# Two-layer cross-attention and experts: the order of the first attention's work on TensorE, in three blocks by the array's shape

## The chip, the cores and the metric
The kernel runs on one core of one Trainium2 chip, in one launch. The metric is device time in microseconds (us) of that core; the median of three runs of the kernel before is 792.72 us (792.16 to 794.59). Inputs and output are fp32.

## The reference, cut to what matters
```
x = x + L0_xattn(ctx, layernorm(x))        # the first attention: 16 heads of 64, 4 batches of 512 queries
x = x + L0_ffn(layernorm(x))               # 8 experts, each row to its best one
x = x + L1_xattn(layernorm(x), ctx)        # 16 heads of 8, keys from ctx alone
x = x + L1_ffn(layernorm(x))               # 8 experts, each row to its best two

def L0_xattn(ctx, latents):                # ctx (4, 32, 128), latents (4, 512, 128)
    kv_in = layer_norm(ctx), lat = layer_norm(latents)
    q = lat @ Wq                           # 128 -> 16 * 64
    k, v = concat([kv_in, lat]) @ Wkv      # 32 + 512 keys
    attn = softmax(q k^T / 8)              # exact, over 544 keys
    return (attn v) @ Wout
```
Only the first attention's order of work changes.

## The kernel before, in words
**Tiling.** The first attention is done pair by pair: two heads of 64 fill 128 partitions, 8 pairs per batch, 4 batches, so 32 pairs (`ALL`); four pairs are a group (`GROUP`), 8 groups. For a pair the kernel makes queries and keys (`qk`, six matmuls of 512 columns over the full 128x128 array, from rounded high and low parts), takes the maximum of each query's scores from the high parts alone (`top`: four tiles of 128 queries x 512 keys for two heads, and a fifth, `t4`, for the 32 context keys; DVE reduces each), turns the maxima into a row (`max_turn`, four transposes, full array; ACT keeps the row in `TOPROW`), makes the scores key tile by key tile (`scores`, four key tiles; each is four steps of two matmuls of 64 rows: high x high, high x low, low x high, and minus the maximum), ACT takes exp into `PT`, POOL adds the key tiles (`PSUMS`), and `pv` multiplies exp by the values (four key tiles, 64-column matmuls over 128 rows, into bank 6). `rows` sums over the keys on TensorE, once per two pairs, into bank 7.

Per group come `context_scores` (32 context keys, both heads, all four pairs, from an unrounded copy `QF` of the queries), `context_sums` and `context_add` (their part of the output, in two halves), `one_over` (the reciprocals of the sums, in four column quarters on DVE, split in a high and a low part by ACT and DVE), `spread` (the reciprocals brought to all partitions by TensorE, two pairs each, DVE multiplies), `out` (times Wout) and `add` (to x). Per batch: layernorm of the next batch (`a_stats`, `a_rstd`, `a_out`, `a_turn`, `a_split`), its `values` (four steps), and the routing of the finished batch (`r0_stats` to `r0_send`).

**The order.** It is written out by hand. `ITERATION` is a list of short names that is run for each pair i; in iteration i stand qk and the maxima of pair i+1 (`qk`, `t0` to `t4`, `mt`), pv of pair i-1 (`p0` to `p3`), the scores of pair i (`s0` to `s3`), and the slots (letters) in which `put` has placed the work of groups and batches. The result is one list, `order_a`; every engine runs its own part of each step in the order of this list, and the engines meet at semaphores. The last pair's rest stands in a list of its own, `rest`.

**Banks.** Each step named in `TAKES_BANKS` gets two PSUM banks, `2 * (place % 3)`, by turns: of three pairs of banks, a step uses the one that the third step before it used. TensorE waits (`claim`) until that one's reader is done: for `scores` ACT's exp, for `top` DVE's reduction, for `qk` DVE's low part of the queries (`QL`), for `max_turn` ACT's copy. `pv` and `rows` take no turning pair.

**Shapes.** A matmul's tile of the array stands in the profile behind the operation: 128*128 for qk, values, transposes, spread, out, r0_turn and r0_run; 128*64 for pv; 64*128 for top and scores; 128*32 for rows; 64*32 and 32*64 for the context.

Lines in the profile: L1407 to L1409 qk and values, L1569 and L1576 top (context: L1576), L1583 max_turn, L1602 scores, L1634 pv, L1689 spread; ACT L838 exp, L732 layernorm, L815 and L816 high parts, L863 the reciprocals' high part; DVE L1225 and L1228 low parts (KL, QL), L1235 and L1237 reductions of top, L1255 reciprocals; POOL L671 additions.

Of the kernel before, what the change touches and what calls it, by code (L numbers as in the profile page):

```python
# [13 lines left out]
P = 128  # L14
# [27 lines left out]
def build(nc, x, ctx, lnm_g, lnm_b, lnl_g, lnl_b, Wq, Wkv, Wout, rw, rb, w1, w2, cq, ckv, cc, Wr, Wg, Wu, Wd, out):  # L42
# [28 lines left out]
    with ExitStack() as stack:  # L71
# [35 lines left out]
        with ExitStack() as queries:  # L107
            QF = queries.enter_context(nc.sbuf_tensor("QF", [P, GROUP, S], F32))
            TOPROW = queries.enter_context(nc.sbuf_tensor("TOPROW", [P, GROUP, S], F32R))
# [47 lines left out]
        with ExitStack() as first:  # L157
            def sb1(name, *shape):
                return first.enter_context(nc.sbuf_tensor(name, [P, *shape], F32R))


            WH = sb1("WH", 3, INNER)
            WL = sb1("WL", 3, INNER)

            XTH = sb1("XTH", 2, S)
            XTL = sb1("XTL", 2, S)

            QH = sb1("QH", 2, S)
            QL = sb1("QL", 2, S)
            KH = sb1("KH", 2, S)  # L170
            KL = sb1("KL", 2, S)

# [82 lines left out]
        for b in range(B):  # L255
# [64 lines left out]
            "E A B PC CA0 C CA1 O0 ADD CS V qk p0 p1 t0 s0 t1 p2 t2 D s1 t3 p3 t4 P0 P2 s2 s3 rows mt O1 OUT "  # L320
            "O2 O3").split()
# [3 lines left out]
        def put(i, at, name, a):  # L325
            beside[i].setdefault(at, []).append((name, a))
        for g in range(2 * B):

            put(GROUP * g + GROUP - 1, "CS", "context_scores", g)
            for half in range(2 if g < 2 * B - 1 else 0):  # L330
                put(GROUP * (g + 1) + 1, "PC", "context_sums", (g, half))
                put(GROUP * (g + 1) + 1, f"CA{half}", "context_add", (g, half))
        for b in range(B + 1):
            i = b * PAIRS
            if 2 <= b:
                put(i, "A", "r0_slot", b - 2)
                put(i, "D", "r0_send", b - 2)
            if b == B:
                break
            if b + 1 < B:  # L340
                put(i, "E", "a_stats", b + 1)
                put(i, "A", "a_rstd", b + 1)
                put(i + 1, "D", "a_out", b + 1)
                put(i + 3, "C", "a_turn", b + 1)
                put(i + 3, "D", "a_split", b + 1)
                for kt in range(KT):
                    put(i + 4 + kt, "V", "values", (b + 1, kt))
            for g in (2 * b - 1, 2 * b):
                if g >= 0:

                    k = GROUP * (g + 1) + 1
                    for c in range(4):
                        put(k, f"O{c}", "one_over", (g, c))
                    put(k + 1, "P0", "spread", GROUP * g)
                    put(k + 1, "P2", "spread", GROUP * g + 2)
                    put(k + 1, "OUT", "out", g)
                    put(k + 2, "ADD", "add", g)
            if b > 0:
                put(i + 4, "E", "r0_stats", b - 1)
                put(i + 4, "A", "r0_rstd", b - 1)  # L360
                put(i + 4, "D", "r0_out", b - 1)
                put(i + 5, "D", "r0_turn", b - 1)
                put(i + 6, "B", "r0_logits", b - 1)
                put(i + 6, "C", "r0_top", b - 1)
                put(i + 7, "A", "r0_hot", b - 1)
                put(i + 7, "D", "r0_run", b - 1)
# [3 lines left out]
        order += first_top[4:] + [("max_turn", 0), ("context_kept", 1), ("counters", 0)]  # L370
# [17 lines left out]
        for at in ITERATION:  # L388
# [6 lines left out]
                ("one_over", (last, 0))] + [("pv", (ALL - 1, kt)) for kt in range(KT)]  # L395
        rest += [("one_over", (last, c)) for c in range(1, 4)] + [("context_sums", (last, 1), 4, 2), ("context_add", (last, 1)),
# [26 lines left out]
        SCORED = {step: i + 1 for i, step in enumerate(scored)}  # L423

# [3 lines left out]
        def context_of(g):  # L428
            return SCORED["context_scores", g]

# [297 lines left out]
        def scalar_program(act):  # L728
# [64 lines left out]
            for name, a, place, banks in order_a:  # L793
# [16 lines left out]
                elif name == "qk":  # L810
# [41 lines left out]
                elif name == "one_over" and a[1] == 0:  # L852
                    g = a[0]
# [63 lines left out]
        def vector_program(dve):  # L917
# [295 lines left out]
            for name, a, place, banks in order_a:  # L1213
# [26 lines left out]
                elif name == "max_turn":  # L1240
# [7 lines left out]
                elif name == "one_over":  # L1248
# [7 lines left out]
                    if c == 3:  # L1256
                        if g == 2 * B - 1:
                            tables(0, True, "rows")
                        dve.wait_ge(s_rech, g + 1)
                        dve.wait_ge(s_rec, 4 * (g + 1))  # L1260
                        dve.tensor_tensor(RECS[64:128, :], REC[0:64, :], RECS[0:64, :].bitcast(F32), ALU.subtract).then_inc(s_recl, 1)
# [125 lines left out]
        def tensor_program(pe):  # L1387
# [129 lines left out]
            for name, a, place, banks in order_a:  # L1517
# [87 lines left out]
                elif name == "context_scores":  # L1605
# [6 lines left out]
                    for step in range(2):  # L1612
                        if step:
                            pe.wait_ge(s_toprow, GROUP * (a + 1))
                        for p in range(GROUP):
                            for h in range(2):
                                r = slice(DH * h, DH * h + DH)
                                lhs = (KCF[r, half * GROUP + p, ctx_b], MINUS[r, 0:M].bitcast(F32))[step]
                                rhs = (QF[r, p, :], TOPROW[r, p, :].bitcast(F32))[step]
# [253 lines left out]
```

## Time and profile before
| | |
|---|---|
| median of 3 runs | 792.72 us |
| span of the profiled execution | 798.2 us |
| TensorE matmuls busy | 713.8 us (89%) |
| VectorE (DVE) | 491.6 us (62%) |
| ScalarE (ACT) | 366.9 us (46%) |
| GpSimd (POOL) | 378.2 us (47%) |

The profile is of one execution. Its span goes from the first to the last instruction; it is the only time of that execution that there is, and the profile adds nothing outside it. It is 5.5 us above the median of the runs, which were taken without the profiler. Busy time counts a matmul from its start to its modelled end, so neighbouring matmuls overlap: distances from start to start say what one costs. The first attention takes from about 15 to 515 us; behind it come the first experts, the second attention and its experts.

### The profile page before, as it was taken

The page shows a single profiled execution, that of the slowest core. Times are in us where ns is not written, and L with a number is a line of the kernel's source. Part 1 is how long each engine was busy: PE and PEld are TensorE (multiplying, and loading weights), DVE is VectorE, ACT ScalarE, POOL GpSimd, SP SyncE. Part 2 cuts the span into 40 slices and gives each one's busy share as a digit, 9 for nine tenths or more (in the row PEclk, how much of TensorE's full clock was granted, in tenths as well). Part 3 has the DMA queues.
Part 4 walks back from the last instruction along what each step waited for, and adds up shares of the span by engine and source line. Part 5 has one row for each costly group of instructions (what it writes and reads, how often), then busy time and mean ns, then how long its engine had stood idle before and what let it go on. Part 6 is the DMA issues. An engine that isn't in the chain of part 4 may idle for free.

```text
span 798.2 us, 13900 instructions
## 1 busy us (share of the span) xinstructions
PE 713.8 (89%) x4626; PEld 414.0 (52%) x4626; DVE 491.6 (62%) x1077; ACT 366.9 (46%) x572; POOL 378.2 (47%) x369
## 2 busy tenths in 40 slices
PE   4899999999999999999999999987995587659991
PEld 4655556545556545555545455454664244326660
DVE  4655484595594875675775666664442477746673
ACT  5465554564654553654554643432332543314440
POOL 6254453553563573464375454524222314765552
PEclk9999999999999999999999999999998688569996
DMA  9999999300000000000030004302111500122224
GB/s 235 163 161 160 158 160 157 43 1 1 1 2 1 6 10 1 1 1 2 1 119 1 1 1 106 119 18 58 36 39 56 174 2 28 37 72 67 81 69 177
DMA packets 69132, 50.45 MB, mean 63 GB/s; under 512 B 4068, under 2 KB 62312, under 8 KB 69064
## 3 DMA queue, kind: packets, MB, share of 16 engines
q1 hardware_dynamic: 65544, 42.30, 29.7%
q0 software_dynamic: 3520, 7.27, 2.8%
q8 instruction: 41, 0.67, 0.4%
q14 instruction: 27, 0.22, 0.1%
HBM read 20.07 MB, written 29.47 MB: 62 GB/s over the span
## 4 chain that ended last, share of the span: by engine, by line
PE 75%; DVE 8%; issue 6%; POOL 4%; ACT 3%; DMA 2%; another core or an unknown queue 1%; SPq 1%; DVEq 0%; POOLq 0%; ACTq 0%
PE PSUM L1602 14%; PE PSUM L1634 13%; PE PSUM L1444 7%; PE PSUM L1569 5%; PE PSUM L1469 4%; PE PSUM L1700 4%; PE PSUM L1403 4%; PE PSUM L1407 3%; PE PSUM L1409 2%; PE PSUM L1408 2%; PE PSUM L1583 2%; PE PSUM L1576 2%; PE PSUM L1620 2%; PE PSUM L1664 2%; POOL results_d L643 2%
## 5 line engine op out<-in xcount | busy, mean ns | idle before, releaser
L838 ACT ACTIVATE PT<-PSUM 128x1024 f32<-128x1024 f32 x128 | 128.7, 1025 | 134.2 <-PE PSUM L1602 133.9
L671 POOL TENSOR_TENSOR PSUMS<-PT 128x1024 f32<-128x1024 f32 x32 | 76.1, 2378 | 210.6 <-ACT PT L838 171.6
L671 POOL TENSOR_TENSOR PSUMS<-PSUMS,PT 128x1024 f32<-128x1024 f32 x62 | 149.7, 2415 | 16.6 <-ACT PT L838 9.7
L1235 DVE TENSOR_REDUCE TOPS<-PSUM 128x2 f32<-128x1024 f32 x128 | 152.0, 1220 | 7.4 <-PE PSUM L1569 7.0
L1634 PE MATMUL PSUM<-PT,BIG 128*64 128x512 f32 x512 | 130.6, 611 | 0.6 <-issue 0.6
L1444 PE MATMUL PSUM<-BIG,XGT 128*128 x170 | 86.5, 614 | 2.4 <-issue 1.6
L1225 DVE TENSOR_TENSOR KL<-PSUM,KH 128x512 fp32r<-128x512 f32 x32 | 22.1, 692 | 68.0 <-ACT KH L816 67.5
L1189 DVE TENSOR_TENSOR SIL<-SIL,PSUM 128x256 f32<-128x256 f32 (+1 forms) x62 | 32.1, 518 | 48.0 <-ACT SIL L758 45.4
L1569 PE MATMUL PSUM<-KH,QH 64*128 64x512 f32 x256 | 58.0, 449 | 3.9 <-DVE QL L1228 3.6
L1634 PEld LDWEIGHTS PSUM<-PT,BIG 128*64 128x64 f32 x512 | 28.4, 135 | 54.0 <-issue 52.5
L1602 PE MATMUL PSUM<-QH,KH 64*128 64x512 f32 x256 | 54.9, 424 | 1.0 <-DVE QL L1228 0.8
L1569 PEld LDWEIGHTS PSUM<-KH,QH 64*128 64x128 f32 x256 | 24.2, 183 | 59.2 <-DVE TOPS L1235 25.1
L758 ACT ACTIVATE SIL<-PSUM 128x256 f32<-128x256 f32 (+1 forms) x62 | 28.7, 463 | 55.1 <-PE PSUM L1444 43.5
L643 POOL DMA_INDIRECT results_d<-YS,IDX x39 | 37.4, 960 | 31.5 <-issue 20.4
L766 ACT ACTIVATE HIDT<-PSUM 128x256 f32<-128x256 f32 (+1 forms) x62 | 28.7, 463 | 51.3 <-PE PSUM L1403 43.0
L1602 PE MATMUL PSUM<-QL,KH 64*128 64x512 f32 x256 | 50.9, 390 | 0.0
L1602 PE MATMUL PSUM<-QH,KL 64*128 64x512 f32 x256 | 50.8, 390 | 0.0
L1602 PE MATMUL PSUM<-TOPROW,MINUS 64*128 64x512 f32 x256 | 50.7, 389 | 0.0
L643 POOL DMA_INDIRECT results_b<-YS,IDX x23 | 22.0, 956 | 47.1 <-DVE YS L1196 44.8
L1274 DVE TENSOR_TENSOR OT<-OT,PSUM 128x1024 f32<-128x1024 f32 x16 | 18.9, 1217 | 34.0 <-PE PSUM L1651 34.0
L1444 PEld LDWEIGHTS PSUM<-BIG,XGT 128*128 128x128 f32 x170 | 28.1, 195 | 15.4 <-issue 15.3
L635 POOL DMA_INDIRECT lists_d<-BIG,SLOT x28 | 27.3, 975 | 10.4 <-issue 9.4
(255 smaller groups left out, 1358.5 us busy)
## 6 DMA issues: line engine op xcount, KB each, us to landing
lists_d<-EMPTY SPq DMA_DIRECT2D x3, 2730.0 KB, 44.7
lists_b<-EMPTY SPq DMA_DIRECT2D x3, 2470.0 KB, 41.7
lists_d<-EMPTY SPq DMA_DIRECT2D x1, 2665.0 KB, 43.9
XG<-lists_d SPq DMA_DIRECT2D x39, 65.0 KB
lists_b<-EMPTY SPq DMA_DIRECT2D x1, 2405.0 KB, 20.6
BIG<-in_L_ffn_w SPq DMA_DIRECT2D x1, 2048.0 KB
W2ALL<-in_L_ffn_w SPq DMA_DIRECT2D x4, 512.0 KB, 6.1
PT<-results_d SPq DMA_DIRECT2D x8, 256.0 KB, 4.9
```

Of the source, the lines that this page charges most:

```text
L643: pool.indirect_dma_start(RES[which], bass.IndirectOffsetOnAxis(ap=IDX[:, g % 8:g % 8 + 1].bitcast(U32), axis=0), YS[:, g % 8, :], None).t ...
L671: pool.tensor_tensor(PSUMS[:, i % 2], PTT[:, i % 2, 0] if kt == 1 else PSUMS[:, i % 2], PTT[:, i % 2, kt], ALU.add).then_inc(s_ps, 1)
L838: act.activation(PTT[:, i % 2, kt], PSUM[:, place:place + 2, :], ACT.Exp, scale=DH ** -0.5).then_inc(s_exp, 1)
L1189: dve.tensor_tensor(sl, sl, up, ALU.mult).then_inc(s_hid, 1)
L1235: dve.tensor_reduce(TOPS[:, c, 0, :], PSUM[:, place:place + 2, :], AX.X, ALU.max).then_inc(s_max, 1)
L1403: last = pe.transpose(PSUM[:, bank, t * P:(t + 1) * P], src(t), IDENT[:, :])
L1444: last = pe.matmul(PSUM[:, bank + n, :], XGT[:, g % 3, :], weights[:, bass.ds(column[which][j], BANK)], start=True, stop=True)
L1469: last = pe.matmul(PSUM[:, bank, 0:D], HIDT[:, g % 2, f * P:(f + 1) * P], weights[:, f * D:][:, bass.ds(column[which][j], D)], start=f == ...
L1569: last = pe.matmul(PSUM[:, place + h, :], QH[r, i % 2, c * P:(c + 1) * P], KH[r, i % 2, :], start=True, stop=True)
L1602: last = pe.matmul(PSUM[:, place + h, :], lhs, rhs, start=step == 0, stop=step == 3)
L1634: last = pe.matmul(PSUM[DH * h:DH * h + DH, 6, :], V[:, b % 2, kt, cols], PTT[:, i % 2, kt, h, :], start=kt == 0, stop=kt == KT - 1)
L1700: last = pe.matmul(PSUM[:, place, t * P:(t + 1) * P], OT[:, (GROUP * a + c) % OTS, t * P:(t + 1) * P], WOUT[:, (GROUP * a + c) % PAIRS, :] ...
```

## The change
The iteration's list is put in another order, and five steps are cut or moved:
- In an iteration come first the steps of the full array (a_turn, r0_turn or r0_run, values, qk of pair i+1, max_turn, spread), then pv of pair i-1 in one piece, then out, rows and context_scores, then the scores of pair i and the maxima of pair i+1 by turns: s0 t0 s1 t1 s2 t2 s3 t3 t4.
- max_turn is now that of pair i, one iteration later in the list; DVE's joining of the five maxima has its own name, `max_joined` (`mj`), and stays at the end of iteration i-1.
- one_over is cut in three: ACT's copy of the sums (`one_half`, H), the reciprocals (one in O of the group's second iteration, one in O and two in R of its third), and the low part (`one_low`, RL, with a wait for the spreads of the group before).
- The slots of the other steps move by up to one iteration; the halves of context_sums stand in two iterations; spread, out and add stand in the group's fourth iteration.
- The unrounded queries get a fifth place (`QF1` beside `QF4`), so that ACT's copy doesn't wait for context_scores that now come later.

No matmul, exp, reduction or addition is added or left out.

```
-            "E A B PC CA0 C CA1 O0 ADD CS V qk p0 p1 t0 s0 t1 p2 t2 D s1 t3 p3 t4 P0 P2 s2 s3 rows mt O1 OUT "
-            "O2 O3").split()
+            "O C V qk mt P0 P2 PC B E A CA R p0 p1 D p2 p3 OUT ADD rows CS s0 t0 s1 t1 H s2 t2 s3 t3 t4 mj RL").split()
 
         for g in range(2 * B):
-            put(GROUP * g + GROUP - 1, "CS", "context_scores", g)
-            for half in range(2 if g < 2 * B - 1 else 0):
-                put(GROUP * (g + 1) + 1, "PC", "context_sums", (g, half))
-                put(GROUP * (g + 1) + 1, f"CA{half}", "context_add", (g, half))
+            k = GROUP * (g + 1)
+            put(k - 1, "CS", "context_scores", g)
+            if g == 2 * B - 1:
+                break
+            for half in range(2):
+                put(k + half, "PC", "context_sums", (g, half))
+                put(k + half, "CA", "context_add", (g, half))
+            put(k, "H", "one_half", g)
+            put(k + 1, "O", "one_over", (g, 0))
+            put(k + 2, "O", "one_over", (g, 1))
+            put(k + 2, "R", "one_over", (g, 2))
+            put(k + 2, "R", "one_over", (g, 3))
+            put(k + 2, "RL", "one_low", g)
+            put(k + 3, "P0", "spread", GROUP * g)
+            put(k + 3, "P2", "spread", GROUP * g + 2)
+            put(k + 3, "OUT", "out", g)
+            put(k + 3, "ADD", "add", g)
         for b in range(B + 1):
             i = b * PAIRS
-            if 2 <= b:
-                put(i, "A", "r0_slot", b - 2)
-                put(i, "D", "r0_send", b - 2)
...
-                put(i, "E", "a_stats", b + 1)
-                put(i, "A", "a_rstd", b + 1)
-                put(i + 1, "D", "a_out", b + 1)
+                put(i + 1, "E", "a_stats", b + 1)
+                put(i + 1, "A", "a_rstd", b + 1)
+                put(i + 2, "D", "a_out", b + 1)
...
-            for g in (2 * b - 1, 2 * b):
-                if g >= 0:
-                    k = GROUP * (g + 1) + 1
-                    for c in range(4):
-                        put(k, f"O{c}", "one_over", (g, c))
-                    put(k + 1, "P0", "spread", GROUP * g)
-                    put(k + 1, "P2", "spread", GROUP * g + 2)
-                    put(k + 1, "OUT", "out", g)
-                    put(k + 2, "ADD", "add", g)
             if b > 0:
                 put(i + 4, "E", "r0_stats", b - 1)
                 put(i + 4, "A", "r0_rstd", b - 1)
-                put(i + 4, "D", "r0_out", b - 1)
-                put(i + 5, "D", "r0_turn", b - 1)
+                put(i + 5, "D", "r0_out", b - 1)
+                put(i + 6, "C", "r0_turn", b - 1)
                 put(i + 6, "B", "r0_logits", b - 1)
-                put(i + 6, "C", "r0_top", b - 1)
-                put(i + 7, "A", "r0_hot", b - 1)
-                put(i + 7, "D", "r0_run", b - 1)
+                put(i + 6, "B", "r0_top", b - 1)
+                put(i + 6, "A", "r0_hot", b - 1)
+                put(i + 7, "C", "r0_run", b - 1)
+                put(i + 7, "A", "r0_slot", b - 1)
+                put(i + 7, "D", "r0_send", b - 1)
...
-                elif at in ("qk", "mt") and i + 1 < ALL:
-                    order.append(("qk" if at == "qk" else "max_turn", i + 1))
+                elif at in ("qk", "mj") and i + 1 < ALL:
+                    order.append(("qk" if at == "qk" else "max_joined", i + 1))
+                elif at == "mt" and i:
+                    order.append(("max_turn", i))
...
+        def query(i):
+            return QF4[:, i % (GROUP + 1), :] if i % (GROUP + 1) < GROUP else QF1[:, :]
...
-                    if a >= GROUP:
-                        act.wait_ge(s_sc, context_of(a // GROUP - 1))
-                    act.activation(QF[:, a % GROUP, :], PSUM[:, place, :], ACT.Copy).then_inc(s_qkh, 1)
+                    if a > GROUP:
+                        act.wait_ge(s_sc, context_of((a - 1) // GROUP - 1))
+                    act.activation(query(a), PSUM[:, place, :], ACT.Copy).then_inc(s_qkh, 1)
...
+                elif name == "one_low":
+                    g = a
+                    dve.wait_ge(s_rech, g + 1)
+                    dve.wait_ge(s_rec, 4 * (g + 1))
+                    if g:
+                        dve.wait_ge(s_bc, 4 * g)
+                    dve.tensor_tensor(RECS[64:128, :], REC[0:64, :], RECS[0:64, :].bitcast(F32), ALU.subtract).then_inc(s_recl, 1)
```

## Rows read from the trace of the kernel before

**Rows 1.** Busy us (instructions) of the engines in two stretches, then TensorE's clock, DMA.
```profile
160.00:260.00 100.00, 99.25 (x684) 56.04 (x680) 66.14 (x89) 53.12 (x76) 49.13 (x24) 1.00 0.01 1
...
600.00:798.00 198.00, 138.17 (x808) 85.92 (x806) 118.68 (x430) 68.79 (x151) 89.74 (x117) 0.79 0.26 77
```

**Rows 2.** Timeline of TensorE, one iteration: start, duration, line, operation, out<-in, count.
```profile
44.19 1.94 PE L1634 MATMUL PSUM<-PT,BIG 128*64 128x512 f32 x8 [0.59 <-issue]
46.05 0.50 PE L1569 MATMUL PSUM<-KH,QH 64*128 64x512 f32 x2
...
47.32 0.40 PE L1569 MATMUL PSUM<-KH,QH 64*128 64x512 f32 x2
47.65 1.08 PE L1634 MATMUL PSUM<-PT,BIG 128*64 128x512 f32 x4
48.66 0.50 PE L1569 MATMUL PSUM<-KH,QH 64*128 64x512 f32 x2
...
51.25 0.62 PE L1576 MATMUL PSUM<-KCH,QH 64*128 64x32 f32 x8
51.72 0.48 PE L1602 MATMUL PSUM<-QH,KH 64*128 64x512 f32 x2
...
53.75 0.65 PE L1583 MATMUL PSUM<-IDENT,TOPT 128*128 128x128 f32 x4
54.16 0.47 PE L1407 MATMUL PSUM<-XTH,WH 128*128 128x512 f32 x1
...
55.72 1.94 PE L1634 MATMUL PSUM<-PT,BIG 128*64 128x512 f32 x8
```

**Rows 3.** Timeline of all engines, a maximum and its reduction; idle time before in brackets.
```profile
31.63 0.42 PE L1569 MATMUL PSUM<-KH,QH 64*128 64x512 f32 x2
...
32.09 1.22 DVE L1235 TENSOR_REDUCE TOPS<-PSUM 128x2 f32<-128x1024 f32 x1 [0.44 <-PE PSUM L1569]
```

**Rows 4.** Timeline of all engines, 286 to 298 us.
```profile
286.47 0.40 PE L1602 MATMUL PSUM<-TOPROW,MINUS 64*128 64x512 f32 x2
286.78 0.68 DVE L1228 TENSOR_TENSOR QL<-PSUM,QH 128x512 fp32r<-128x512 f32 x1
286.91 1.02 ACT L838 ACTIVATE PT<-PSUM 128x1024 f32<-128x1024 f32 x1 [1.66 <-PE PSUM L1602]
287.38 4.61 DVE L1235 TENSOR_REDUCE TOPS<-PSUM 128x2 f32<-128x1024 f32 x4
...
287.61 0.50 PE L1569 MATMUL PSUM<-KH,QH 64*128 64x512 f32 x2 [0.74 <-DVE QL L1228]
287.83 1.64 ACT L732 ACTIVATE NRM<-X,NMR,RSTD 128x128 f32<-128x128 f32 x4
...
292.85 2.56 DVE L1255 RECIPROCAL REC<-REC 64x128 f32<-64x128 f32 x3
...
294.43 5.18 POOL L671 TENSOR_TENSOR PSUMS<-PSUMS,PT 128x1024 f32<-128x1024 f32 x2 [0.42 <-ACT PT L838]
...
295.65 0.62 ACT L863 ACTIVATE RECS<-REC 64x512 fp32r<-64x512 f32 x1
295.79 0.40 PE L1409 MATMUL PSUM<-XTH,WL 128*128 128x512 f32 x1
...
298.00 0.68 DVE L1228 TENSOR_TENSOR QL<-PSUM,QH 128x512 fp32r<-128x512 f32 x1
```

**Rows 5.** Timeline of TensorE around two spreads.
```profile
242.84 0.62 PE L1576 MATMUL PSUM<-KCH,QH 64*128 64x32 f32 x8
243.39 1.19 PE L1689 MATMUL PSUM<-RECS,SPREAD 128*128 128x512 f32 x4
244.51 0.51 PE L1602 MATMUL PSUM<-QH,KH 64*128 64x512 f32 x2
```

**Rows 6.** Waits: who waited for whom, total us, times, longest.
```profile
PE PSUM L1569 <- DVE QL L1228: 3.6, 5, 0.7
```

**Rows 7.** Timeline of DVE at a routing step.
```profile
267.28 2.39 DVE L1061 CAST SLOT<-RSM 128x4 int32<-128x4 f32 x1
```

More of the change, by code:

```diff
@@ L107, in build @@
         with ExitStack() as queries:
-            QF = queries.enter_context(nc.sbuf_tensor("QF", [P, GROUP, S], F32))
+            QF4 = queries.enter_context(nc.sbuf_tensor("QF4", [P, GROUP, S], F32))
             TOPROW = queries.enter_context(nc.sbuf_tensor("TOPROW", [P, GROUP, S], F32R))
@@ L171, in build @@
             KL = sb1("KL", 2, S)
+            QF1 = first.enter_context(nc.sbuf_tensor("QF1", [P, S], F32))
         W2ALL = sb("W2ALL", E * F_B)
@@ L360, in build @@
                 put(i + 4, "A", "r0_rstd", b - 1)
-                put(i + 4, "D", "r0_out", b - 1)
-                put(i + 5, "D", "r0_turn", b - 1)
+                put(i + 5, "D", "r0_out", b - 1)
+                put(i + 6, "C", "r0_turn", b - 1)
                 put(i + 6, "B", "r0_logits", b - 1)
-                put(i + 6, "C", "r0_top", b - 1)
-                put(i + 7, "A", "r0_hot", b - 1)
-                put(i + 7, "D", "r0_run", b - 1)
+                put(i + 6, "B", "r0_top", b - 1)
[3 more added lines that the diff above has]
+                put(i + 7, "D", "r0_send", b - 1)
         first_top = [("top", (0, c)) for c in range(TOPS_OF)]
         order = [("qk", 0), ("context_keys", 1)] + first_top[0:2] + [("values", (0, 0))] + first_top[2:4] + [("values", (0, 1))]
-        order += first_top[4:] + [("max_turn", 0), ("context_kept", 1), ("counters", 0)]
+        order += first_top[4:] + [("max_joined", 0), ("max_turn", 0), ("context_kept", 1), ("counters", 0)]
         instead = [[("values", (0, 2))], [], [("values", (0, 3))], [("context_values", 0), ("spread_rounded", 0)]]
@@ L394, in build @@
         rest = [("e_tables", 0), ("kv_copies", 0), ("context_sums", (last, 0), 2, 2), ("rows", ALL - 1), ("context_add", (last, 0)),
-                ("one_over", (last, 0))] + [("pv", (ALL - 1, kt)) for kt in range(KT)]
-        rest += [("one_over", (last, c)) for c in range(1, 4)] + [("context_sums", (last, 1), 4, 2), ("context_add", (last, 1)),
+                ("one_half", last), ("one_over", (last, 0))] + [("pv", (ALL - 1, kt)) for kt in range(KT)]
+        rest += [("one_over", (last, c)) for c in range(1, 4)] + [("one_low", last), ("context_sums", (last, 1), 4, 2), ("context_add", (last, 1)),
                  ("e_tables", 2), ("masks", 0)]
@@ L851, in scalar_program @@
                     act.activation(OT[:, i % OTS, :], PSUM[:, 6, :], ACT.Copy).then_inc(s_ot, 1)
-                elif name == "one_over" and a[1] == 0:
-                    g = a[0]
+                elif name == "one_half":
+                    g = a
                     act.wait_ge(s_rows, GROUP // 2 * (g + 1))
@@ L1239, in vector_program @@
                                           AX.X, ALU.max).then_inc(s_max, 1)
-                elif name == "max_turn":
+                elif name == "max_joined":
                     dve.wait_ge(s_max, TOPS_OF * (a + 1))
@@ L1255, in vector_program @@
                     dve.reciprocal(REC[0:64, cols], REC[0:64, cols]).then_inc(s_rec, 1)
[L1256 to L1261, printed above, removed]
+                    if c == 3 and g == 2 * B - 1:
+                        tables(0, True, "rows")
+                elif name == "one_low":
+                    g = a
+                    dve.wait_ge(s_rech, g + 1)
[3 more added lines that the diff above has]
+                    dve.tensor_tensor(RECS[64:128, :], REC[0:64, :], RECS[0:64, :].bitcast(F32), ALU.subtract).then_inc(s_recl, 1)
                 elif name == "spread":
@@ L1618, in tensor_program @@
                                 lhs = (KCF[r, half * GROUP + p, ctx_b], MINUS[r, 0:M].bitcast(F32))[step]
-                                rhs = (QF[r, p, :], TOPROW[r, p, :].bitcast(F32))[step]
+                                rhs = (query(GROUP * a + p)[r, :], TOPROW[r, p, :].bitcast(F32))[step]
                                 last = pe.matmul(PSUM[p * M:(p + 1) * M, place + h, :], lhs, rhs, start=step == 0, stop=step == 1)
```

## The prediction
> **What bounds the kernel now.** I read the busy time by stretch first. In 160 to 260 us, inside the first attention, TensorE is busy 99.25 of 100 us at granted clock 1.00 (its 2.4 GHz level); DVE has 66, ACT 53 and POOL 49 [rows 1]. Then the list of waits: there a maximum waits for DVE's QL in five places, 3.6 us in all, and TensorE for hardly anything else [rows 6]. So every TensorE nanosecond saved is one of the span, and every wait added is one too, while the others have a third or more to spare on average. Whether they have the time at the right moment only the timeline can tell, so I read it last: start to start on TensorE it shows what a change of the array's shape costs, and engine by engine how long a pair of PSUM banks is away.
>
> **One plain iteration, before.** It runs from 44.19 to 55.72: 11.53 us [rows 2]. Two pv key tiles take 1.86, one takes 1.01, so one is 0.215 x 4 = 0.86 plus 0.15 on entering. A maximum with the four steps of a score tile behind it takes 1.27: five pairs of matmuls at 0.232 and 0.11 on entering. A maximum that pv follows takes 0.33, so leaving is 0.09 or 0.10. The context maximum takes 0.47 (I take 0.45 where nothing is entered), the last two score tiles 2.03, the transposes of the maximum 0.41, the projection 1.56. A trip from scores to pv and back thus costs about 0.35.
>
> The Trainium skill, "TensorEngine Tiling (Array Packing)", section "Key Properties", says that a change of tiling mode drains the array. The 0.35 us per trip agree with it, and by that rule alone the change would be a gain (the first rival).
>
> **What it saves.** The new order has 3 shape changes in a cycle where the old has 7. One block of pv: 16 x 0.215 + 0.15 = 3.59. One block of scores: 0.11 + 20 x 0.232 + 0.45 + 0.09 = 5.29. Transposes and projection as before, 1.97. Sum 10.85 against 11.53. I take 0.70 (between this 0.68 and two trips' 0.70); times 31 iterations that have maxima, 21.7 us.
> - The spreads stood between scores: 0.55 - 0.47 on going there, 1.12 - 4 x 0.232 = 0.19 on going back, 0.11 on entering scores again: 0.38 [rows 5]. Seven of them, three r0_turn and three r0_run go to the full-array block: 13 x 0.38 = 4.9.
> - The last iteration has no maxima but loses two trips: 0.7.
> - The five waits for QL stand at the second maximum; that now comes after all of pv: 3.6 [rows 6].
> - out, context_scores, rows and context_sums keep as many shape changes as they had: 0.
> Saved: 30.9 us.
>
> **What it adds: the pair of banks that isn't back.** Score tiles and maxima take turns on three pairs of banks, so each waits for the one three places before it. Before, 0.86 us of pv, which takes no turning bank, stood behind each second of them. Now nine follow each other. What a pair costs, from the rows: a score tile's last step to the start of its exp 0.44, the exp 1.02 [rows 4]. A maximum's start to DVE's 0.46 [rows 3], the reduction 1.22 (four in a row take 4.61, so 1.13 apart), the end on DVE to the next matmul 0.15 [rows 4]; for the end on ACT I take the same 0.15. A matmul that waited has no weights loaded ahead, for which I add 0.08 (an estimate from the 0.11 of an entry).
> With 0 at the start of s0: s0's last step starts at 0.80, its exp runs 1.24 to 2.26. t0 starts at 1.04, its reduction runs 1.50 to 2.72. s1 runs 1.27 to 2.20, its exp 2.40 to 3.42. t1 wants s0's pair: 2.41, a wait of 0.21. s2 wants t0's: 2.87, not 2.72. t2 3.87. s3 wants t1's, whose reduction ends at 4.17: 4.32, not 4.11. t3 5.33. t4 wants t2's: 5.70, not 5.56. The projection wants s3's, whose exp ends at 6.55: it starts at 6.70 and not at 5.29. So 1.41 us of waiting, say 1.40, in an iteration that saves 0.70: 12.23 for 11.53. Times 31: 43.4.
> Bounds. Three pairs of banks can't do better than their time away: a score tile 0.69 + 0.44 + 1.02 + 0.15 = 2.30, a maximum 1.83, together 4.13, a third of it 1.38 per two, against 1.16 on TensorE: four times 0.22 is 0.9 (28 us in all). Upwards, every hand-back 0.1 later makes 1.9 (59 us). I take 1.40 since each of its pieces has a row.
>
> The Trainium skill says the same from the other side: "TensorEngine Tiling (Array Packing)", section "PSUM Bottleneck", has it that packing speeds up TensorE and not the emptying of PSUM. It speaks against this change; no run yet shows that it holds in this block.
>
> **What else it adds.**
> - P2 stands three places behind the projection, so it wants the projection's banks, which QL gives back. From the last projection matmul's start to QL's end are 298.00 + 0.68 - 295.79 = 2.89 [rows 4], plus 0.15. Only 0.23 + 0.41 + one spread's 0.46 lie between: 1.94 of waiting. Six times (the seventh has no projection): 11.6. Before, scores and maxima stood there. Bounds: 1.7 to 3 each, as DVE comes to KL at once or behind a reciprocal.
> - ACT's queue: where a reciprocal's high part (R) and the normalising of the next batch (D) meet, in iterations 10 and 18, ACT does projection copies, waits for the two reciprocals (0.85 each, from 2.56 for three), copies 0.62, normalises 1.64 and copies pv [rows 4] before exp of s0. That comes some 1.8 later than its tile: 3.6 for both, bounds 0 and 6. In iterations 6, 14, 22 and 30 R alone, behind the routing's small operations, costs some 0.5: 2.0.
> - The tail: rows of the last pair wait for one addition on POOL (2.6 each, from 5.18 for two [rows 4]). It starts with s1's exp, now in a block of 3.9 us with 1 us of context_sums behind it: 0.9 late.
> - POOL's three additions, 7.8 us, run from 3.42 to some 11.2 of an iteration of 12.2, and rows read them at the end: hidden by 1 us; without that slack each microsecond would count 15 times. The one_half copy lies between two exps, the reductions of the stats and the additions to OT between QL and the first maximum: 0. Loading the last expert weights starts some 5 us later against the end of the attention, with over 20 us before their use: 0.
> Added: 43.4 + 11.6 + 5.6 + 0.9 = 61.5 us. Less 30.9: **30.6 us slower.** The profiled execution has a span of 798.2 and would have 828.8; the median of the runs is 5.5 lower, 792.7, so 823.3. I give 823.
>
> **The rivals.**
> - The saving stays and the block's waits don't come: 792.7 - 30.9 + 18.1 (the other added terms) = 780. It would be so if a matmul could start before its banks are given back, or if exp and reduction ran in less than their rows. For it speaks that shape changes are the only thing TensorE loses now; against it that each pair is claimed before its tile. The sign turns where a block waits less than (30.9 - 18.1) / 31 = 0.41 us. 7%.
> - The block waits only what three pairs of banks need, 0.9, and the pieces overlap better than I lay them: 823 - 31 x 0.5 = 808. 12%.
> - DVE becomes late in the iterations with side work (adding to OT, stats, reciprocals: 16 of them), and t0's reduction starts 0.7 later: 823 + 11 = 834. For it: a DVE operation on 128x4 numbers once took 2.39 us [rows 7]; against: from QL to the first reduction are over 2 us. 14%.
> - The short waits lower the granted clock in the attention, as it is lower in the late stages (0.79 in 600 to 798 us, a mix of the levels 1.2 and 2.4 GHz [rows 1]). With a mean of 0.9 over 430 us: 870. Against: the waits of 0.7 for QL left it at 1.00 [rows 1, 6]. 2%.
>
> **How the numbers follow.** My forecast has 65%: 823. The range 806 to 838 takes in the 0.9 (28 us) and most of the way to the 1.9 as well as the second and third rival, and leaves out the first and the last and some of the tails. About 0.3% (2.4 us) is what can be told from no change here. Faster: the first rival, 0.07. Within it: 0.02, what lies between 0.33 and 0.49 us of waiting per block (0.08 x 31 = 2.4). Slower: 0.91.
>
> **What would show it.** TensorE starts s0 to t4 without pv between; before t1, s2, s3 and t4 it waits 0.1 to 0.3 us, by turns for ACT's exp and DVE's reduction, and before the projection about 0.5 for exp. P2 waits 1.9 us for QL six times. Busy TensorE falls from 99% to about 88% of the stretch, with clock 1.00. A batch of eight takes some 131 us, where it took 124. The experts and the second attention keep their length. I am wrong if t1 to t4 follow without idle time, if the eight iterations take 124 us or less, or if the difference stands behind the attention.

## The result, and where the time went

The changed kernel took 837.84 us (median of 4 runs, 834.38 to 839.27) beside 793.65 for the kernel before (4 runs, 792.16 to 794.69). The ratio is 1.0543, 95% interval [1.0512, 1.0574]: 44.2 us slower where I had forecast 30.6. The time lies 0.2 us below the upper end of my range (806 to 838).

The profiled execution has a span of 837.5 us. I measured from the start of the second iteration's transposes (L1583 before, L1594 after) to the end of the last pv: 41.57 to 515.4 before, which is 473.8 us; 45.26 to 562.5 after, 517.2 us, so 43.4 us more. Ahead of it lie 3.7 us more, one of them the first iteration's own; behind it the rest took 282.9 and 275.0 us, and in later runs of kernels with the same rest 281 to 290, so that part says nothing of the change. The eight iterations from the tenth transposes to the eighteenth took 123.84 and now 138.02; I call them the batch below. I had said 131.

First the busy times by stretch, the view of [rows 1]: busy us (instructions) of TensorE, its weight loads, DVE, ACT and POOL, then TensorE's granted clock, DMA share and GB/s.

```profile
180.00:240.00 60.00, 55.82 (x373) 31.98 (x372) 35.65 (x50) 30.20 (x46) 27.99 (x15) 1.00 0.00 1
...
262.00:278.00 16.00, 12.07 (x44) 5.72 (x44) 10.32 (x21) 3.51 (x7) 7.07 (x4) 0.79 0.02 5
...
530.00:545.00 15.00, 11.02 (x52) 4.94 (x50) 10.97 (x21) 2.77 (x4) 8.96 (x5) 0.77 0.01 4
```

TensorE was busy 99% of such a stretch and is now at 93%, where I had said 88%. Busy time runs to a matmul's modelled end, some 0.16 us past the start of the next one, so most of a wait of 0.2 us doesn't show in it; the sums below therefore go from start to start. In three short stretches (the third, 400 to 416 us, isn't printed: 12.57 of 16 at 0.79), 130 to 138 us apart, it is at 73 to 79%, and its clock is a mix of its two levels: cut finer, it is 1.00 up to 269.9 us, 0.50 (1.2 GHz) to 276.7 and 1.00 again behind. Nothing like that stood in the kernel before: there the 16 us from 262 show 16.00 busy at 1.00. Next the waits on TensorE from 60 to 560 us (who waited for whom, total us, times, longest), the view of [rows 6]:

```profile
PE PSUM L1418 <- ACT PT L846: 8.5, 20, 0.5
PE PSUM L1700 <- DVE QL L1236: 7.1, 6, 1.6
PE PSUM L1594 <- DVE PLACE L1058: 4.1, 2, 2.1
PE PSUM L1414 <- ACT PT L846: 2.8, 6, 0.6
PE PSUM L1700 <- DVE PLACE L1058: 2.4, 1, 2.4
...
PE PSUM L1675 <- POOL PSUMS L679: 0.7, 1, 0.7
```

The projection (L1418) waits for exp (L846) and the spread (L1700) for QL, both forecast. The five waits of a maximum for QL that stood before [rows 6] are gone, as forecast. The two rows with PLACE (L1058) I did not have. Then TensorE's timeline through one block of scores (L1613) and maxima (L1580), from s0 to the projection; it answers to the score rows of [rows 2]:

```profile
298.58 0.50 PE L1613 MATMUL PSUM<-QH,KH 64*128 64x512 f32 x2
...
299.61 0.39 PE L1580 MATMUL PSUM<-KH,QH 64*128 64x512 f32 x2
299.84 0.40 PE L1613 MATMUL PSUM<-QH,KH 64*128 64x512 f32 x2
...
300.98 0.50 PE L1580 MATMUL PSUM<-KH,QH 64*128 64x512 f32 x2
301.41 0.50 PE L1613 MATMUL PSUM<-QH,KH 64*128 64x512 f32 x2
...
302.42 0.42 PE L1580 MATMUL PSUM<-KH,QH 64*128 64x512 f32 x2
302.89 0.49 PE L1613 MATMUL PSUM<-QH,KH 64*128 64x512 f32 x2
...
303.88 0.43 PE L1580 MATMUL PSUM<-KH,QH 64*128 64x512 f32 x2
304.24 0.62 PE L1587 MATMUL PSUM<-KCH,QH 64*128 64x32 f32 x8
305.28 0.47 PE L1418 MATMUL PSUM<-XTH,WH 128*128 128x512 f32 x1 [0.42 <-ACT PT L846]
```

Read the gaps between starts: with 0.23 a pair, t1 comes 0.21 late, s2 0.20, s3 0.24 and t4 0.13, and the projection waits 0.42. The longer first matmul (0.50 against 0.39) is the one that waited. The block takes 6.70, the figure that I had laid out step by step, and it takes 6.65 to 6.77 in 28 of the 31 iterations.

The other rows are of one place. This is all engines from 262 to 278 us, at the transposes of iteration 15, answering to [rows 5] for the spreads and to [rows 7] for the small DVE step:

```profile
261.88 5.15 POOL L679 TENSOR_TENSOR PSUMS<-PSUMS,PT 128x1024 f32<-128x1024 f32 x2
...
263.23 0.17 DVE L1254 TENSOR_REDUCE TOPT<-TOPS 128x8 f32<-128x16 f32 x1
...
264.83 2.25 DVE L1037 TENSOR_TENSOR ROUT<-ROUT,RSM 128x32 f32<-128x32 f32 x1
...
267.77 0.19 DVE L1058 TENSOR_TENSOR PLACE<-RUN,PSUM 128x32 f32<-128x32 f32 x1
268.06 0.63 PE L1594 MATMUL PSUM<-IDENT,TOPT 128*128 128x128 f32 x4 [2.06 <-DVE PLACE L1058]
...
269.87 0.68 DVE L1236 TENSOR_TENSOR QL<-PSUM,QH 128x512 fp32r<-128x512 f32 x1
...
270.65 1.19 PE L1700 MATMUL PSUM<-RECS,SPREAD 128*128 128x512 f32 x2 [1.49 <-DVE QL L1236]
271.77 6.10 PE L1645 MATMUL PSUM<-PT,BIG 128*64 128x512 f32 x16
277.81 0.60 PE L1711 MATMUL PSUM<-WOUT,OT 128*128 128x128 f32 x3
```

Two pauses of 2.06 and 1.49 us, 2.6 apart, and behind them a pv block that takes 6.04 (to the next start) where the plain one takes 3.59. The last is what I had given 2%.

### The profile page after: what moved, and what is told of

It reads as the page before. It is cut to its first block and busy times, and to the rows that moved or that the text cites. A ratio compares the mean times of both kernels' runs of the same rounds, so it can differ in the third digit from the quotient of the medians.

```text
span 837.5 us, 13900 instructions
## 1 busy us (share of the span) xinstructions
PE 726.8 (87%) x4626; PEld 436.5 (52%) x4626; DVE 493.9 (59%) x1077; ACT 367.3 (44%) x572; POOL 378.4 (45%) x369
## 5 line engine op out<-in xcount | busy, mean ns | idle before, releaser
L1243 DVE TENSOR_REDUCE TOPS<-PSUM 128x2 f32<-128x1024 f32 x128 | 156.3, 1224 | 116.1 <-PE PSUM L1580 112.4
L846 ACT ACTIVATE PT<-PSUM 128x1024 f32<-128x1024 f32 x128 | 130.7, 1025 | 61.1 <-PE PSUM L1613 58.0
L1645 PE MATMUL PSUM<-PT,BIG 128*64 128x512 f32 x512 | 122.8, 623 | 0.0
L1645 PEld LDWEIGHTS PSUM<-PT,BIG 128*64 128x64 f32 x512 | 35.2, 142 | 76.2 <-issue 76.2
L859 ACT ACTIVATE OT<-PSUM 128x512 f32<-128x512 f32 x32 | 19.0, 593 | 110.3 <-PE PSUM L1711 66.3
L1613 PE MATMUL PSUM<-QH,KH 64*128 64x512 f32 x256 | 61.0, 464 | 2.1 <-DVE TOPS L1243 0.7
L1580 PE MATMUL PSUM<-KH,QH 64*128 64x512 f32 x256 | 56.3, 420 | 2.4 <-ACT PT L846 1.3
L1613 PE MATMUL PSUM<-TOPROW,MINUS 64*128 64x512 f32 x256 | 52.8, 391 | 0.0
L1613 PE MATMUL PSUM<-QL,KH 64*128 64x512 f32 x256 | 52.7, 390 | 0.0
L1613 PE MATMUL PSUM<-QH,KL 64*128 64x512 f32 x256 | 52.7, 390 | 0.0
L1613 PEld LDWEIGHTS PSUM<-QH,KH 64*128 64x128 f32 x256 | 26.0, 183 | 49.9 <-issue 26.2
L1580 PEld LDWEIGHTS PSUM<-KH,QH 64*128 64x128 f32 x256 | 26.8, 185 | 21.3 <-ACT PT L846 14.5
L1455 PEld LDWEIGHTS PSUM<-BIG,XGT 128*128 128x128 f32 x170 | 28.9, 201 | 16.3 <-issue 16.2
## 6 DMA issues: line engine op xcount, KB each, us to landing
lists_b<-EMPTY SPq DMA_DIRECT2D x1, 2405.0 KB, 22.4
```

What stands on the lines that cost most here:

```text
L846: act.activation(PTT[:, i % 2, kt], PSUM[:, place:place + 2, :], ACT.Exp, scale=DH ** -0.5).then_inc(s_exp, 1)
L1243: dve.tensor_reduce(TOPS[:, c, 0, :], PSUM[:, place:place + 2, :], AX.X, ALU.max).then_inc(s_max, 1)
L1455: last = pe.matmul(PSUM[:, bank + n, :], XGT[:, g % 3, :], weights[:, bass.ds(column[which][j], BANK)], start=True, stop=True)
L1580: last = pe.matmul(PSUM[:, place + h, :], QH[r, i % 2, c * P:(c + 1) * P], KH[r, i % 2, :], start=True, stop=True)
L1613: last = pe.matmul(PSUM[:, place + h, :], lhs, rhs, start=step == 0, stop=step == 3)
L1645: last = pe.matmul(PSUM[DH * h:DH * h + DH, 6, :], V[:, b % 2, kt, cols], PTT[:, i % 2, kt, h, :], start=kt == 0, stop=kt == KT - 1)
```

## The experiments

All times are medians beside the kernel before on the same chip. Its own median was 800.22 beside inter, spread1, run_late and pc_one, 799.51 beside after_half, before_half, combo and best, and 804.59 beside fill, two_blocks, later_first and both. The expectations are written on the first chip's scale (before 793.65, after 837.84), so compare differences, not times. "Way" is the distance from the second transposes to the last pv's end: 473.8 us before, 517.2 after.

**inter: pv back between the tiles, the rest of the change kept (out, rows, context_scores, D and H shift with it).**
```diff
-"... R p0 p1 D p2 p3 OUT ADD rows CS s0 t0 s1 t1 H s2 t2 s3 t3 t4 mj RL"
+"... R p0 p1 OUT ADD CS t0 s0 t1 p2 t2 D s1 t3 p3 t4 s2 s3 rows H mj RL"
```


> The changed kernel, but pv goes back between the score tiles (p0 p1 .. t0 s0 t1 p2 t2 s1 t3 p3 t4 s2 s3); the rest of the new order stays. Theory A (three turning pairs of banks aren't back in time): the block's waits of some 1.4 us in 31 iterations go (43 us), the two trips between shapes come back (31 x 0.70 = 22): 838 - 21 = 817. Rival B (the loss stands in the new order of the DVE and ACT queues, not in the block): the trips come back and nothing goes: 860.


Measured 822.58, ratio 1.0290 [1.0242, 1.0337], +22.4 us; way 490.0, batch 130.12. So rival B falls: the way is 27.2 us shorter than after, about 21 of it forecast for the block (waits less shape changes). The rest has other causes: the waits for PLACE (6.5 us after) are down to 0.2, and the clock is at 1.00 over the whole way, where after had three slow pv blocks. Against the kernel before 16.2 us remain. Their largest waits are P2's for QL, and one for TOPS that this order brings anew:

```profile
PE PSUM L1700 <- DVE QL L1236: 9.9, 6, 1.6
PE PSUM L1580 <- DVE TOPS L1243: 4.1, 7, 1.1
```

No row with exp is left, and no pv block is slow. PLACE comes in time: the DVE step ahead of it (L1037), which took 2.25 us at 264.83 after, took 0.19 here (at 254.99), 2.06 less, and the transposes had waited 2.06.

**spread1: the spreads ahead of the projection.**
```diff
-"O C V qk mt P0 P2 PC ..."
+"O C V P0 P2 qk mt PC ..."
```


> The changed kernel with both spreads ahead of the projection and the transposes, so that the second no longer asks for the projection's banks. Theory A: the waits for QL go, 7.1 us in the profile after: 831; if TensorE's lower granted clock around the seventh iteration of each batch (pv took 6.0 and 5.3 us where it takes 3.6) is a consequence of these pauses, another 6 us go: 825. Rival: the clock falls without them (by the other pause at the routing's counts, or by chance): 831, and the slow pv blocks stay.


Measured 847.76, 1.0607 [1.0567, 1.0646], +47.5. The waits for QL are gone, and in their place stand:

```profile
PE PSUM L1700 <- DVE RECS L1272: 9.0, 7, 2.8
...
PE PSUM L1700 <- DVE PLACE L1058: 4.8, 2, 2.4
```

The spread now comes before DVE has written the RECS that it reads. QL's wait had covered a second one behind it. Both expectations (831 and 825, so 7 or 13 us less) missed. The batch is 2.1 shorter (135.96), the way 2.8, less than the runs can tell: the medians say 3 us more, and the part behind the attention varies by more than that from execution to execution.

**run_late: r0_run behind the transposes, in the place B.**
```diff
-put(i + 7, "C", "r0_run", b - 1)
+put(i + 7, "B", "r0_run", b - 1)
```


> The changed kernel with the routing's counts (r0_run) behind the transposes of the maximum and not ahead of the projection, so the transposes no longer ask for its banks and DVE makes KL and QL first. Theory A: the waits for PLACE go, 6.5 us in the profile after: 831; with the slow pv blocks, if they follow from this pause, 825. Rival: a new wait in its place, since DVE's small operations now stand ahead of the first reduction: 836 to 838.


Measured 837.10, 1.0463 [1.0416, 1.0510], +36.9; batch 133.58. That is 4.44 less than after, and two rows give it: the transposes' wait of 2.06 is gone, and the pv block is 2.45 shorter, although one pause of 1.64 still stands just ahead of it. Over the whole kernel it is 7 us less, as theory A had it without the clock; one wait of 1.4 for TOPT is new. TensorE's timeline:

```profile
267.90 0.70 PE L1700 MATMUL PSUM<-RECS,SPREAD 128*128 128x512 f32 x2 [1.64 <-DVE QL L1236]
...
268.90 3.65 PE L1645 MATMUL PSUM<-PT,BIG 128*64 128x512 f32 x16
```

One slow block (5.35, at 402.46) stays in another batch.

**pc_one: both halves of context_sums in one iteration, as before.**
```diff
-put(k + half, "PC", "context_sums", (g, half))
+put(k + 1, "PC", "context_sums", (g, half))
```


> The changed kernel with both halves of context_sums in one iteration again. Theory A: a half took 1.02 us after, both together took 1.04 before, so dividing them costs 1.0 in each of seven groups: 838 - 7 = 831. Rival (DVE's two additions to OT then come between QL and the first reduction and delay it): 837 to 839.


Measured 861.95, 1.0759 [1.0698, 1.0820], +61.7: the worst of all, where I expected 7 less than after. The second half claims the banks of QL:

```profile
242.37 1.53 PE L1662 MATMUL PSUM<-PTC,VC 32*64 32x512 f32 x8 [1.14 <-DVE QL L1236]
243.82 4.86 PE L1645 MATMUL PSUM<-PT,BIG 128*64 128x512 f32 x16
```

Seven such waits make 7.9 us, and they also undo the saving itself: with a pause between them the halves don't run side by side. In the second group the first half starts at 171.12, the second at 173.35, and pv at 174.37: 3.25 us, against 2.04 for two halves apart (and 1.04 for sixteen matmuls together before, and in best). That is 1.2 us more seven times, 8.4 in all. Ten pv blocks are slow (4.86 to 5.92), some 17 us where after had 5.9; the mean clock of the span is 0.925. The two make 19.5 of the 19.9 us by which the way grew. It is the trap of P2 a second time, and it leaves the price of divided context_sums to the rows: no run takes it away alone.

**after_half and before_half: from the third pair on the maxima read 256 of a tile's 512 columns, and exp does 256; the matmuls stay whole.** They ask what the blocks are worth where exp and reduction are not in the way.
```diff
-dve.tensor_reduce(TOPS[:, c, 0, :], PSUM[:, place:place + 2, :], AX.X, ...)
+dve.tensor_reduce(TOPS[:, c, 0, :], PSUM[:, place:place + 2, 0:BANK // 2], AX.X, ...)
...
-act.activation(PTT[:, i % 2, kt], PSUM[:, place:place + 2, :], ACT.Exp, ...)
+n = BANK if i < 2 else BANK // 2
+act.activation(PTT[:, i % 2, kt, :, 0:n], PSUM[:, place:place + 2, 0:n], ACT.Exp, ...)
```


> The changed kernel with less to read from the banks: DVE reduces 256 of each 512 columns of a maximum (the context maximum as before) and ACT takes exp of 256 of 512 columns from the third pair on (the output is not the reference's). TensorE's work is unchanged. A pair of banks is back some 0.6 us earlier. Theory A (banks): the block's waits go (43 us), and the fewer shape changes show for the first time: 838 - 43 = 795, block of scores 5.3 us start to start. Rival C (the shape changes themselves cost nothing, the 0.35 us of a trip is only moved): block waits go, but an iteration keeps 11.5: 815 or more.

> The kernel before with the same halved reductions and exps (the output is not the reference's). TensorE never waited for them: 792 to 794 by theory A, with the plain iteration at 11.53 us. If it becomes faster by over 5 us, my reading that TensorE alone sets its time is wrong.


after_half: 812.79, 1.0184 [1.0158, 1.0211], +13.3; way 485.6. before_half: 800.50, 1.0014 [0.9991, 1.0037]. So the kernel before has nothing to win from a faster exp or reduction (its way is 1.7 us shorter), and of the changed kernel's loss 31 us go with them. The block, s0 to the projection:

```profile
281.92 0.50 PE L1614 MATMUL PSUM<-QH,KH 64*128 64x512 f32 x2
...
282.95 0.40 PE L1581 MATMUL PSUM<-KH,QH 64*128 64x512 f32 x2
...
286.44 0.40 PE L1581 MATMUL PSUM<-KH,QH 64*128 64x512 f32 x2
286.67 0.51 PE L1588 MATMUL PSUM<-KCH,QH 64*128 64x32 f32 x8
287.38 0.47 PE L1419 MATMUL PSUM<-XTH,WH 128*128 128x512 f32 x1 [0.20 <-ACT PT L847]
```

5.46 with a wait of 0.20, or 5.26 without: the 5.29 that I had for a block that waits for nothing. The saving in shape changes is real, and rival C (815 or more, 21 above before) falls. Theory A expected 1 us above before, though, and 13 were measured. The block gives 1.25 us each time, 39 in all and not 43; the waits at iteration 15 grew (TensorE comes earlier to the same late DVE), and four pv blocks are slow:

```profile
PE PSUM L1701 <- DVE QL L1237: 6.2, 6, 1.6
PE PSUM L1595 <- DVE PLACE L1059: 5.8, 2, 2.9
```

**combo: spread1, run_late and pc_one together.**
```diff
-"O C V qk mt P0 P2 PC ..."
+"O C V P0 P2 qk mt PC ..."
-put(k + half, "PC", "context_sums", (g, half))
+put(k + 1, "PC", "context_sums", (g, half))
-put(i + 7, "C", "r0_run", b - 1)
+put(i + 7, "B", "r0_run", b - 1)
```


> The changed kernel with the three small edits together: spreads ahead of the projection, r0_run behind the transposes, both halves of context_sums in one iteration; pv stays in one piece. Theory A: 7.1 + 6.5 + 7 + 6 (clock) = 27 less: 811. If the clock's fall is by chance: 817. What is left against 793 is the block's waits less the shape changes saved.


Measured 848.99, 1.0650 [1.0610, 1.0690], +49.5, where I expected +18. The waits for RECS (10.8 us, 7 times) and of L1662 for QL (7.9, 7 times) are both there, and one pv block is slow instead of ten. The waits for PLACE are gone, as in run_late. The three edits don't add up, since two of them (the spreads, and the second half) move a step next to another slow hand-back.

**best: the transposes first, the spreads ahead of the projection, context_sums behind it, pv between the tiles.**
```diff
-"O C V qk mt P0 P2 PC B E A CA R p0 p1 D p2 p3 OUT ADD rows CS s0 t0 s1 t1 H s2 t2 s3 t3 t4 mj RL"
+"mt O C P0 P2 V qk B OUT ADD CS PC E A CA R p0 p1 t0 s0 t1 p2 t2 D s1 t3 p3 t4 mj s2 s3 rows H RL"
```
(with run_late and pc_one)


> Pv between the score tiles as in the kernel before, and the rest in the new grouping: transposes of the maximum first, then the full-array steps, spreads, values, projection, out, context_scores and context_sums in one iteration; r0_turn and r0_run among them. Theory A: the kernel before less the 13 trips of spreads and routing turns (4.9) and the QL waits (3.6): 785. Rival: the full-array steps now bring new waits for DVE (out for the spread's multiplications, the first maximum's banks for QL): 793 to 800.


Measured 815.15, 1.0204 [1.0161, 1.0247], +15.6; way 486.3, batch 128.21. It is the fastest version that keeps the full-array steps together, and still slower than before; theory A had it 8 faster, the rival at most 7 slower. The additions to OT (L1285) now stand ahead of the first reduction, and the scores wait for them:

```profile
PE PSUM L1580 <- DVE TOPS L1243: 8.6, 10, 1.3
PE PSUM L1613 <- DVE OT L1285: 4.6, 7, 1.5
```

The rival's wait, out (L1711) for the spread's multiplications, is there too: 3.5 us, 4 times.

**fill: is it the pauses that lower the clock?** Eight matmuls into bank 6, read by nobody, ahead of three transposes, and six ahead of the second spread.
```diff
+if name == "max_turn" and a in (15, 23, 31):
+    keep_busy(6, 8)
+if name == "spread" and a in (10, 18, 26):
+    keep_busy(6, 6)
```


> The changed kernel with idle time of TensorE filled around the seventh iteration of a batch: eight matmuls of 512 columns into pv's bank ahead of the transposes of iterations 15, 23 and 31, and six ahead of the second spread of those iterations (their results are overwritten by pv). The waits for PLACE and QL stay what they are, only the array is busy in them. If the pauses of 2.1 and 1.5 us lower the granted clock: pv takes 3.6 again (not 6.0 and 5.3), a batch takes 138.0 - 2.5 = 135.5, some 6 us less in all. Rival (the clock falls for another reason): pv stays slow, and the batch takes 138 or more.


Measured 843.11, 1.0462 [1.0400, 1.0524], +38.5; way 510.0, 7.2 less than after, batch 2.85 less. The medians alone can't tell the two kernels apart (the intervals of fill and after overlap); the way can. The three stretches that hold the same work:

```profile
260.00:276.00 16.00, 15.31 (x87) 10.48 (x87) 10.56 (x21) 3.81 (x7) 7.25 (x5) 1.00 0.02 5
396.00:412.00 16.00, 15.68 (x86) 10.92 (x86) 9.75 (x21) 3.09 (x6) 7.39 (x5) 1.00 0.03 10
525.00:540.00 15.00, 13.89 (x94) 9.51 (x98) 9.55 (x21) 1.77 (x4) 8.62 (x7) 1.00 0.03 10
```

Clock 1.00 in all three, and no slow block: the three pv take 3.58 to 3.59 us. Work that computes nothing, put into time that was idle anyway, made the work behind it faster. At these three places the cause is shown: the pauses, not the work behind them.

**two_blocks, later_first, both: can part of the idea serve the kernel before?** Two score tiles side by side and one trip less; the first reciprocal of every odd group behind the maxima; and both.
```diff
-"... qk p0 p1 t0 s0 t1 p2 t2 D s1 t3 p3 t4 P0 P2 s2 s3 rows mt O1 OUT O2 O3"
+"... qk p0 p1 t0 t1 p2 p3 t2 D s0 s1 t3 P0 P2 s2 t4 s3 rows mt O1 OUT O2 O3"
```
```diff
-put(k, f"O{c}", "one_over", (g, c))
+put(k, "O1" if c == 0 and g % 2 else f"O{c}", "one_over", (g, c))
```


> The kernel before with one trip between shapes less in each iteration: pv in two blocks of two, the order p0 p1 t0 t1 p2 p3 t2 s0 s1 t3 s2 t4 s3. By what the runs have shown (a trip 0.35, and a tile waits only if its pair of banks is less than 1.6 to 2.3 us old) 31 x 0.35 = 11 us go, and t3, s2 and t4 may wait 0.1 to 0.4 us together: 3 to 11 us faster, a batch of 121 to 123 instead of 123.8. Rival: the waits are as large as the trip, 0, or more with side work on DVE: up to 5 us slower.

> The kernel before with the first reciprocal of every second group behind the maxima (beside the other three) and not ahead of KL and QL. The waits of 0.74 for QL at iterations 9, 17 and 25 go: a batch takes 123.1 instead of 123.8, and the kernel is 2 us faster, at the edge of what can be told. Rival: the low part of the reciprocals comes later and a spread waits: 0.

> The last two together: a batch of 120 to 122.5, the kernel 5 to 13 us faster than before; if two blocks of pv bring waits of their own, no more than 2 us faster or slower.


two_blocks: 814.63, 1.0104 [1.0058, 1.0151], +10.0; batch 126.23, where I expected 3 to 11 faster or at most 5 slower. Behind pv's second block now stand seven score tiles and maxima in a row (t2 s0 s1 t3 s2 t4 s3), and that is enough to wait: the waits are for the addition to OT and for exp, with 1.5 us more for TOPS.

```profile
PE PSUM L1602 <- DVE OT L1267: 3.6, 7, 0.5
PE PSUM L1602 <- ACT PT L838: 3.0, 3, 1.6
```

later_first: 820.23, 1.0189 [1.0140, 1.0239], +15.6, where I expected 2 less or nothing. Four reciprocals now stand in a row on DVE, and in ACT's queue the copy to RECS that needs them stands ahead of the projection's own copies. All engines:

```profile
174.56 3.38 DVE L1255 RECIPROCAL REC<-REC 64x128 f32<-64x128 f32 x4
177.97 0.63 ACT L863 ACTIVATE RECS<-REC 64x512 fp32r<-64x512 f32 x1 [4.17 <-DVE REC L1255]
...
179.71 0.80 PE L1569 MATMUL PSUM<-KH,QH 64*128 64x512 f32 x2 [4.09 <-ACT KH L816]
...
180.27 0.66 PE L1602 MATMUL PSUM<-QH,KH 64*128 64x512 f32 x2
```

Three waits of 4.1 make 12.3 us, and behind each the matmuls run slow (0.66 for 0.40 a pair). both: 829.50, 1.0303 [1.0259, 1.0348], +24.9, about the sum of the two and far from the expected gain. None of the twelve beat the kernel before.

## Why the prediction was right, and by how much it was short

The sign and its mechanism held: the block waits for its banks as laid out, and P2 waits where I said. That the time still fell within the range is partly luck: it did so by 0.2 us, terms that I had too large (P2, ACT's queue) made room for causes that I had at nothing or at 2%, and those causes are as large as two thirds of the forecast. Measured over the way and the first iteration together, the change costs 44.7 us; my terms, each with what the traces show:

- **The block of scores and maxima.** Foreseen 6.70 for 5.29, 1.41 of waiting, and 12.23 for the plain iteration. Measured 6.70, and 12.28 from projection to projection (43.79 to 56.07). So 0.75 net times 31 is 23.2, where I had 21.7. Three pairs of banks turn no faster than exp and reduction give them back. The Trainium skill, "TensorEngine Tiling (Array Packing)", section "PSUM Bottleneck", has it that packing speeds up TensorE and not the emptying of PSUM. The trace agrees that the emptying sets the pace here: the projection waits 20 times for exp. The rival in which the saving stays without waits had the saving right (after_half: 5.26 for a block that waits for nothing) and the waits wrong.
- **P2 behind the projection.** Foreseen 11.6, measured 7.1 for QL and two of 0.4 for XT: 7.9. Where nothing waits ahead of it, it waits 1.64 (135.52), for which I had 1.94; where the first spread has already waited for XT (0.42 at 197.27) or for RECS (0.34 at 471.56), or the transposes for PLACE, 0.97 to 1.49 are left. The size was off, not the place.
- **ACT's queue.** Foreseen 5.6, measured 1.0: the blocks of iterations 10 and 18 take 7.2 instead of 6.7, with a wait of 0.54 at t1 (190.04), and those of R alone aren't longer. I had left out that in even iterations rows stand ahead of s0 (1.0 us, 186.15 to 187.14), and that is time for ACT.
- **The tail.** Foreseen 0.9, measured 0.71.
- **What is saved.** The waits for QL (3.6) are gone. (The five stand in 60 to 560 us, not all in the 100 us of [rows 1], as my wording has it.) For the spreads (4.9) and the last iteration (0.7) I have no measurement.

These make 23.2 + 7.9 + 1.0 + 0.7 - 4.9 - 3.6 - 0.7 = 23.6. The 21 us that I did not have:

- **"out, context_scores, rows and context_sums keep as many shape changes as they had: 0."** This is the step that failed. context_sums went from seven blocks of 16 matmuls and two of 8 to sixteen of 8. Before, 16 took 1.04 (the first two lines, of before). After, 8 take 1.02 (the last two):

```profile
217.12 1.11 PE L1651 MATMUL PSUM<-PTC,VC 32*64 32x512 f32 x16
218.16 0.50 PE L1407 MATMUL PSUM<-WH,XTH 128*128 128x512 f32 x1
...
218.85 1.09 PE L1662 MATMUL PSUM<-PTC,VC 32*64 32x512 f32 x8
219.87 2.37 PE L1645 MATMUL PSUM<-PT,BIG 128*64 128x512 f32 x10
```

  So a half costs as much as a whole, and seven more blocks are 7.1 us. The kernel before had this price in its tail, where two halves stand alone (507.97, and the next step at 508.98). I had read only shape changes and not durations. In my terms: a term put at nothing that cost 7.1.
- **r0_run's pair of banks.** I moved it to the front of the iteration in "what it saves" and did not ask who stands three places behind it. The transposes do, twice, and a spread once: 2.06, 2.08 and 2.39, 6.5 us. The wait is long because a DVE step on 32 columns (L1037) took 2.25, 2.25 and 2.23 us just then. Where it took 0.19, in inter, with the same three steps behind r0_run, 0.2 of these waits are left.
- **The clock.** Given 2%, and imagined as a lowering over the whole attention. It came in three places only: pv blocks of 6.04, 5.29 and 5.29 for 3.59, so 5.9 us, and the second spreads ahead of them take 1.12 for 0.63, 1.5 more. fill takes both away. My argument against was that waits of 0.7 had left the clock at 1.00; the new waits are up to 2.4 us long and come in twos (2.06 and 1.49, 2.08 and 0.97, 0.75 and 2.39).

Together 21.0. With 1.5 us of two more waits that I had not foreseen (RECS 1.1, TOPT 0.4) and the 23.6 above that is 46.1, where 44.7 were measured. The 1.4 us too many are open; the savings without a measurement may be larger than I had them.

The third rival (DVE late at side work, 834) was close in time and had a part of the truth: DVE is late, though not for t0's reduction but for the banks of r0_run.

What stays open: inter's 16.2 us over before are, by rows, 10.7 us more waiting (QL, TOPS and OT, less what before waited) and 7.1 for the halves, less the 4.9 foreseen at the spreads; 3.3 have no row. Nor can I say from these runs which pauses lower the clock. run_late has one of 1.64 with a full-speed block 1 us behind it; inter has six of 1.64 and keeps 1.00; spread1 has one of 2.40 before 268.02 and then pv at full speed; pc_one has 1.14 and then 4.86.

## What to carry to other kernels

Before grouping steps that share a few buffers, lay out one cycle with hand-back times: from last write to release and back. If the cycle of the buffers (here 4.13 us for a score tile and a maximum, over three pairs of banks 1.38, against 1.16 of matmuls) is longer than the work between, the other work interleaved there was not a cost but the cover. Whenever a step is moved, ask of each of its buffers who comes next at the same place in the turn and how late its reader is; that one question would have found P2, r0_run, and the second half in pc_one and combo. Spread1 adds another: what else does the step read, and is that ready? When a step is split, price the pieces by a row of a piece, not by the whole divided. And look at what a step meets in its new place: r0_run was harmless where no long addition ran on POOL.

## What the hardware showed that I had not expected

- Eight matmuls of 32x64 weights and 512 columns take 1.02 us alone and sixteen take 1.04, where they fill twice as much of the array. With a wait of 1.14 between the halves, sixteen take 3.25.
- Pauses lower TensorE's granted clock for the next few microseconds: after 2.06 and 1.49 us a 16-matmul pv block took 6.04 instead of 3.59, with the clock at 0.79 over 16 us. Useless matmuls in the pauses kept it at 1.00.
- A DVE step on 128x32 numbers (L1037) took 2.25 us while POOL did an addition of 128x1024. It ended at 267.08, POOL's addition at 267.03; in spread1 the pair ended at 267.04 and 267.00, and all nine of the slow ones in after, spread1 and fill end within 0.06 us of an addition. In inter, run_late and combo no addition ran beside this step, and it took 0.18 to 0.19 each time, as in the kernel before (0.18 at 262.80):

```profile
262.80 0.18 DVE L1029 TENSOR_TENSOR ROUT<-ROUT,RSM 128x32 f32<-128x32 f32 x1
```

  So the addition goes with the delay in both directions. It isn't smallness alone: the joining of the maxima (L1254, at 263.23 above) is as small, ran beside the addition just before and took 0.17. Why one waits and the other doesn't, no run shows; none was made for it.
